# A conditioned mixture of experts on one core: seven pieces of work put in other places

## The chip, the core and the metric

The kernel runs on one core of a Trainium2 chip. The time is the device time of one execution in microseconds (us), and the aim is a smaller one. The core has five engines, each with its own queue that it works through in order: PE (TensorE, the matrix products), ACT (ScalarE), DVE (VectorE), POOL (GpSimd) and SP (SyncE, which here only issues transfers). They wait for one another through semaphores. A matrix product consists of a weight load (PEld) and the product itself (PE).

## What is computed

1024 tokens of 256 features are first conditioned: a dense 256x256 product, to which a low-rank product (rank 16, one of eight adapters per sequence of 32 tokens) is added. Behind it a mixture of eight experts works on the result, two experts for each token.

```python
def cond(x, W, A, Bm, scalings, adapter_idx):      # x: (32, 32, 256)
    H = jnp.einsum('btd,od->bto', x, W)
    xa = jnp.einsum('btd,brd->btr', x, A[adapter_idx])
    delta = jnp.einsum('btr,bor->bto', xa, Bm[adapter_idx])
    return H + delta * scalings[adapter_idx][:, None, None]

def ffn(x, w_gate, w1, w2, w3):                    # E = 8, H = 256, I = 704
    routing = softmax_integer(xf @ w_gate.T)       # fixed-point table of exp
    top_w, top_i = jax.lax.top_k(routing, 2)
    combine = zeros.at[arange(T)[:, None], top_i].add(top_w / top_w.sum(-1, keepdims=True))
    for e in range(E):
        h = jax.nn.silu(xf @ w1[e].T) * (xf @ w3[e].T)
        out = out + combine[:, e:e + 1] * (h @ w2[e].T)

out = x + ffn(cond(x, ...), ...)
```

## The kernel before

**Precision.** Products are made from a value split in two: a high part in a rounded 32-bit form and a low part, the rest. A product is hi·lo + hi·hi + lo·hi. ACT makes the high parts by copies (`copy`, L559, one line for all of them), DVE or POOL the low parts by a subtraction. So each operand passes ACT, then DVE (or POOL), then PE.

**First stage (to some 30 us).** PE makes the adapter products, the router's logits (two halves of 512 tokens) and turns them; DVE picks two experts for each token (a chain of small instructions, L767 to L782, whose ninth sets `picked_ready`). The conditioned rows are made in eight tiles of 128 tokens, `base(t)` (six matmuls: four at L1076, two at L1082) and `low_rank(t)` (three, L1093 to L1095); two tiles make a batch, which ACT copies out (`c_copy`) and stores (L574). Between the batches PE counts the picks ahead of each token, the ranks (one matmul at L1151, eight at L1155). From the ranks DVE makes the positions of the rows (L787 to L815), and PE the source of each row (L1179). Rows are grouped by expert into 23 slots of 128. Slot 0 is gathered by matmuls (`first_rows`, L1170); for slots 1 to 22 POOL issues indirect loads (`gather`, L460), the first when DVE has written `src_i` (L835).

**Second stage, the slots.** Each slot has three items i = 3s + j. PE's order for an item: `gate_up(i)` (L1210 four times, L1219 twice), then for one j the turn of the next slot's rows (`turn_slot(s + 1)`, L1188, two transposes that wait for that slot's gather), `turn_hidden(i - 1)` (L1226), `down(i - 2)` (L1247 to L1249; L1241 and L1242 in a slot's last). `turned_at(s)` gives j = 1 for all slots but slot 1, which `LATE_SLOTS` puts at j = 2. Behind a turn ACT makes `xs_hi` and DVE `xs_lo` (L876), and the first product of the next slot waits for both. From slot 1 on the expert's address is a register; ahead of each such product stand register instructions on PE's queue. For each item ACT makes silu (L613, or L617 and L618), DVE the product `hid` (L890, or L895 and L897), ACT `h_hi` and DVE `h_lo` (L905). A slot's result lies in one bank, `ya`; DVE copies it out (`slot_out`, L911, semaphore `y_out`), and the first `down` of the next slot waits for that.

**Weights.** SP loads an expert's weights in three pieces into `raw` (L390; experts 1 and 3 go to other places). For expert 0 the high parts are `expert_hi(0, k)` on ACT and the low parts `first_lo` (L726, piece 0 in halves) and `expert_lo` (L859) on DVE. The first halves of `raw` are free for expert 2 when these are done (`raw_free`).

**The tail.** Slots 0 to 20 are scattered by POOL to DRAM (`scatter`, L482, the s-th not before item s + 43 has its `hid`; `destinations()`, L842 to L852 on DVE, makes the targets) and come back token by token: SP waits for all scatters and issues four loads (L416). ACT scales the first choice (`scale_first`, L638), DVE adds the second (`mix`, L922), PE transposes the sum into the output banks (L1277). Slots 21 and 22 go another way: ACT and DVE split their scaled result (`direct_hi`, L644, and the same `slot_out`, L914), and PE multiplies it with a 0/1 matrix `hot_out`, which POOL makes (L550, two instructions, semaphore `places_ready`) (L1264). DVE adds x (L1010, four instructions) and SP stores (L420, four transfers).

The parts of this order that the change touches are all written out by hand: no scheduler moves them.

## Time and profile before

| | |
|---|---|
| time, median of 3 runs | 202.05 us (201.3 to 202.57) |
| the profiled execution | 201.05 us, of it span 199.3 us |
| PE busy | 192.5 us (97%) |
| PEld, POOL, DVE, ACT busy | 169.6, 130.3, 108.2, 82.5 us |
| chain that ended last | PE 86%, DMA 5%, DVE 4%, issue 1%, SPq 1%, ACT 1% |
| granted clock of PE | 0.997 |

The span runs from the first to the last instruction; 1.75 us of the profiled execution lie around it. A timeline row gives start, length (both us), engine, line, operation, tiles, count, and in brackets how long the engine had been idle and what ended that. Ends of matmuls are modelled and overlap the next one's start, so spacing is read from starts. "issue" is idle time in which nothing that the profile shows was waited for.

### The profile page before, as it was taken

Reading aid. Unit: us, or ns where it says so; the run is one execution under the profiler, and the core shown is the slowest. Engines: PE = TensorE matmul, PEld = TensorE weight load, DVE = VectorE, ACT = ScalarE, POOL = GpSimd, SP = SyncE. Lnnn points to the kernel's source line nnn. Section 1 sums busy time; section 2 is a strip of 40 time slices with the busy share of each in tenths; the row PEclk is TensorE's granted clock in tenths of the full one; section 3 lists DMA queues with packets and bytes.
Section 4 is the critical chain, followed back from the end, with each engine's and each line's share of the span. In section 5 each row is a group of like instructions: output and inputs, shape, how many; then the busy total and the mean of one; then the engine's idle time right before and its main releaser. Section 6 shows DMA issues by size and latency. Waiting matters only on the chain.

```text
span 199.3 us, 3883 instructions
## 1 busy us (share of the span) xinstructions
PE 192.5 (97%) x1209; PEld 169.6 (85%) x1209; DVE 108.2 (54%) x308; ACT 82.5 (41%) x225; POOL 130.3 (65%) x116
## 2 busy tenths in 40 slices
PE   7998999989999999999999999999999999999992
PEld 6677998778899888989988998899889889988861
DVE  0777898874545644435443553345675435543673
ACT  3756583587643323432333333234323333332740
POOL 8300008569898699999999999998544455418500
PEclk9999999999999999999999999999999999999998
DMA  4999522999993114183364356007312111101915
GB/s 130 348 378 386 189 105 68 333 356 361 359 361 117 58 53 132 48 277 99 109 201 169 109 192 189 13 3 250 120 54 54 54 61 60 67 30 53 358 41 212
DMA packets 14419, 32.67 MB, mean 164 GB/s; under 512 B 2400, under 2 KB 7648, under 8 KB 14272
## 3 DMA queue, kind: packets, MB, share of 16 engines
q1 hardware_dynamic: 11008, 25.70, 37.9%
q0 software_dynamic: 2128, 5.64, 8.8%
q10 hardware_dynamic: 1264, 1.07, 1.6%
q8 instruction: 12, 0.20, 0.4%
q14 instruction: 7, 0.06, 0.1%
HBM read 25.45 MB, written 6.96 MB: 163 GB/s over the span
## 4 chain that ended last, share of the span: by engine, by line
PE 86%; DMA 5%; DVE 4%; issue 1%; SPq 1%; ACT 1%; ACTq 0%; DVEq 0%; POOL 0%; POOLq 0%
PE gu L1210 27%; PE gu L1219 14%; PE ya L1247 7%; PE ht L1226 7%; PE ya L1248 6%; PE ya L1249 6%; DMA rows<-expert_rows 4%; PE ya L1018 3%; PE xt L1188 2%; PE gu L1076 2%; DMA expert_rows<-rows,dst_i 1%; PE ya L1242 1%; PE ya L1241 1%; PE gu L1264 1%; PE ya L1170 1%
## 5 line engine op out<-in xcount | busy, mean ns | idle before, releaser
L1210 PE MATMUL gu<-w_all,xs_hi 128*128 (+2 forms) x276 | 70.7, 377 | 0.3 <-issue 0.3
L890 DVE TENSOR_TENSOR hid<-gu,sg 128x256 f32<-128x256 f32 x46 | 19.5, 424 | 62.2 <-ACT sg L613 62.1
L1210 PEld LDWEIGHTS gu<-w_all,xs_hi 128*128 128x128 f32 x276 | 46.7, 188 | 4.8 <-issue 0.5
L613 ACT ACTIVATE sg<-gu 128x256 f32<-128x256 f32 x46 | 17.7, 385 | 73.2 <-PE gu L1219 73.2
L466 POOL TENSOR_TENSOR w_all<-raw,w_all 128x1024 fp32r<-128x1024 f32 (+2 forms) x14 | 43.9, 3147 | 3.8 <-DVE w_all L872 3.7
L460 POOL DMA_INDIRECT rows<-cond_rows,src_i x22 | 24.4, 1109 | 27.4 <-DVE src_i L835 22.9
L1219 PE MATMUL gu<-w_all,xs_lo 128*128 (+1 forms) x138 | 40.5, 375 | 0.0
L1247 PE MATMUL ya<-w_all,h_hi 128*128 (+1 forms) x115 | 38.4, 334 | 0.6 <-DVE rows L911 0.5
L482 POOL DMA_INDIRECT expert_rows<-rows,dst_i x21 | 20.3, 965 | 22.8 <-DVE hid L890 12.0
L1248 PE MATMUL ya<-w_all,h_hi 128*128 (+1 forms) x115 | 32.5, 283 | 0.0
L1249 PE MATMUL ya<-w_all,h_lo 128*128 (+1 forms) x115 | 32.3, 281 | 0.0
L1219 PEld LDWEIGHTS gu<-w_all,xs_lo 128*128 128x128 f32 x138 | 25.6, 188 | 3.9
L905 DVE TENSOR_TENSOR h_lo<-ht,h_hi 128x256 fp32r<-128x256 f32 x69 | 28.6, 414 | 0.0
L559 ACT ACTIVATE h_hi<-ht 128x256 fp32r<-128x256 f32 x69 | 26.7, 387 | 0.0
L1226 PE MATMUL ht<-ident,hid 128*128 128x128 f32 x138 | 26.3, 272 | 0.0
L1247 PEld LDWEIGHTS ya<-w_all,h_hi 128*128 128x128 f32 x115 | 21.7, 189 | 2.6 <-issue 1.5
L1226 PEld LDWEIGHTS ht<-ident,hid 128*128 128x128 f32 x138 | 18.6, 140 | 4.0
L1248 PEld LDWEIGHTS ya<-w_all,h_hi 128*128 128x128 f32 x115 | 21.9, 190 | 0.0
L1249 PEld LDWEIGHTS ya<-w_all,h_lo 128*128 128x128 f32 x115 | 21.7, 189 | 0.0
L515 POOL CAST w_all<-raw 128x1024 fp32r<-128x1024 f32 (+2 forms) x12 | 16.8, 1398 | 0.8 <-POOLq L510 0.8
L617 ACT ACTIVATE sg<-gu 128x128 f32<-128x128 f32 x23 | 6.4, 279 | 23.0 <-PE gu L1219 23.0
L895 DVE TENSOR_TENSOR hid<-gu,sg 128x128 f32<-128x128 f32 x23 | 6.7, 292 | 13.7 <-ACT sg L618 13.6
(192 smaller groups left out, 260.7 us busy)
## 6 DMA issues: line engine op xcount, KB each, us to landing
raw<-expert_weights SPq DMA_DIRECT2D x6, 896.0 KB, 4.8
raw<-expert_weights SPq DMA_DIRECT2D x6, 640.0 KB
raw<-expert_weights SPq DMA_DIRECT2D x6, 512.0 KB, 4.8
expert_rows<-zeros SPq DMA_DIRECT2D x1, 2048.0 KB, 14.4
rows<-expert_rows SPq DMA_DIRECT2D x4, 512.0 KB, 5.3
x<-x_t SPq DMA_DIRECT2D x4, 256.0 KB, 4.6
cond_rows<-c_rows ACTq DMA_DIRECT2D x4, 256.0 KB, 2.1
raw<-x_t SPq DMA_DIRECT2D x1, 1024.0 KB, 4.9
```

Source lines behind the costliest of these rows:

```text
L460: nc.gpsimd.indirect_dma_start(out=rows[:, s, :], out_offset=None, in_=c_dram[:, :], in_offset=bass.IndirectOffsetOnAxis(ap=src_i[:, s:s + ...
L466: return nc.gpsimd.tensor_tensor(lo_part(e, cols), from_raw(e)[:, cols], as_f32(hi_part(e, cols)), ALU.subtract)
L482: nc.gpsimd.indirect_dma_start(out=y_dram[:, :], out_offset=bass.IndirectOffsetOnAxis(ap=dst_i[:, s:s + 1], axis=0), in_=rows[:, s, :], in ...
L559: return nc.scalar.activation(out, in_, ACT.Copy)
L890: nc.vector.tensor_tensor(hid[i % HBUFS][:, :].rearrange("p (a b) -> p a b", b=P), bank[:, :].rearrange("p (a k b) -> p a k b", k=2, b=P)[ ...
L905: nc.vector.tensor_tensor(h_lo[i % HBUFS][:, :], ht[i % 2][:, 0:2 * P], as_f32(h_hi[i % HBUFS][:, :]), ALU.subtract).then_inc(h_lo_ready, 1)
L1210: nc.tensor.matmul(out, stay_hi[:, kc * P:(kc + 1) * P], moving(at, part + first + kc * P, n), start=kc == 0 and part == HI_COLS, stop=False)
L1219: last = nc.tensor.matmul(out, stay_lo[:, kc * P:(kc + 1) * P], moving(at, first + kc * P, n), start=False, stop=kc == KC - 1)
L1226: last = nc.tensor.transpose(ht[i % 2][:, q * P:(q + 1) * P], hid[i % HBUFS][:, q * P:(q + 1) * P], ident[:, :])
L1247: nc.tensor.matmul(out, stay_hi, w_l, start=j == q == 0, stop=False)
L1248: nc.tensor.matmul(out, stay_hi, w_h, start=False, stop=False)
L1249: last = nc.tensor.matmul(out, stay_lo, w_h, start=False, stop=False)
```

## The change

1. **Ranks.** `base(3)` is issued ahead of the rank matmuls on PE, not behind them.
2. **Expert 0.** On ACT the high part of piece 0 is made ahead of the router's weights; piece 1 is split in two (`SECOND_PARTS`, 1024 and 768 columns, with a semaphore of its own, `second_hi_ready`), the first ahead of the second half's `xa_hi`, the second where the whole piece stood. On DVE the first half of piece 0's low part goes ahead of `xa_lo(1)`, and the first part of piece 1's goes ahead of the routing chain; the 768 columns stay where the 1792 stood. `highs_of` counts the high parts, one fewer, for the other waits.
3. **Slot 1's turn.** `LATE_SLOTS` is empty: slot 1 is turned at j = 1 like the others, on PE, ACT and DVE.
4. **Destinations.** `destinations()` moves from item 3 to item 46 on DVE.
5. **`hot_out` of slot 21** is made ahead of the last scatter on POOL, that of slot 22 behind it as before.
6. **The eviction of slot 22.** On ACT `direct_hi(22)` goes ahead of `scale_first(2)`; on DVE `mix(2)` goes behind `slot_out(22)`.

```diff
@@ -34,6 +34,8 @@
+SECOND_PARTS = [slice(2 * ITEM_COLS, 4 * ITEM_COLS), slice(4 * ITEM_COLS, DOWN_AT)]
 HI_PIECES = [PIECES[0], PIECES[1], slice(DOWN_AT, HI_COLS)]
@@ -67,7 +69,7 @@
-LATE_SLOTS = (1,)
+LATE_SLOTS = ()
@@ -278,6 +280,7 @@
         raw_free = [sem(f"raw_free{k}") for k in range(len(PIECES) - 1)]
+        second_hi_ready = sem("second_hi_ready")
         second_ready = sem("second_ready")
@@ -344,6 +347,10 @@
             return 0 if e in (STAGED, STAGED_LOW) else e - (e > STAGED) - (e > STAGED_LOW)
+        def highs_of(e, k):
+            return len(PIECES) * e + k + 1 - (e > 0 or k > 0)
@@ -490,14 +497,14 @@
                 for k in range(len(PIECES) - 1):
-                    pool.wait_ge(whi_ready, len(PIECES) * e + k + 1)
+                    pool.wait_ge(whi_ready, highs_of(e, k))
                     ins = low(e, k)
...
                     fetch(e, n)
-                pool.wait_ge(whi_ready, len(PIECES) * (e + 1))
+                pool.wait_ge(whi_ready, highs_of(e, 2))
                 pool.wait_ge(third_ready, e - 1)
@@ -534,7 +541,16 @@
+            def make_places(l):
+                nc.gpsimd.tensor_scalar(hot_out[:, l, :], tokens, place[:, l:l + 1], None,
+                                        ALU.is_equal).then_inc(places_ready, 1)
             for s in range(SENT):
+                if s == SENT - 1:
+                    pool.wait_ge(pool_step, 4)
+                    for l in range(DIRECT - 1):
+                        make_places(l)
                 pool.wait_ge(hid_done, s + PACE)
@@ -545,10 +561,7 @@
-            pool.wait_ge(pool_step, 4)
-            for l in range(DIRECT):
-                nc.gpsimd.tensor_scalar(hot_out[:, l, :], tokens, place[:, l:l + 1], None,
-                                        ALU.is_equal).then_inc(places_ready, 1)
+            make_places(DIRECT - 1)
@@ -565,6 +578,10 @@
                     copy(hi_part(e, HI_PIECES[k]), from_raw(e)[:, HI_PIECES[k]]).then_inc(whi_ready, 1)
+            def first_hi_part(cols):
+                act.wait_ge(raw_in[1], RAW_LOADS[1])
+                copy(hi_part(0, cols), raw[:, cols]).then_inc(second_hi_ready, 1)
@@ -586,16 +603,17 @@
             copy(xa_hi[0][:, :], xa[0][:, :]).then_inc(xa_hi_ready, 1)
+            expert_hi(0, 0)
             act.wait_ge(g_done, 1)
...
             copy(g_both[:, :, 0:EXPERTS], g_at.rearrange("p (c e) -> p c e", e=EXPERTS)).then_inc(g_hi_ready, 1)
+            first_hi_part(SECOND_PARTS[0])
             act.wait_ge(xa_masked, 2)
             copy(xa_hi[1][:, :], xa[1][:, :]).then_inc(xa_hi_ready, 1)
-            expert_hi(0, 0)
             for h in range(HALVES):
...
                 copy(logits[:, tok_of(h)], logits_at[h]).then_inc(logits_out, 1)
-            expert_hi(0, 1)
+            first_hi_part(SECOND_PARTS[1])
             c_copy(0)
@@ -677,8 +695,8 @@
+            direct_hi(SLOTS - 1)
             scale_first(2)
-            direct_hi(SLOTS - 1)
             scale_first(3)
@@ -723,6 +741,11 @@
                 dve.wait_ge(whi_ready, 1)
+                return nc.vector.tensor_tensor(lo_part(0, cols), raw[:, cols], as_f32(hi_part(0, cols)), ALU.subtract)
+            def second_piece_lo(n):
+                cols = SECOND_PARTS[n]
+                dve.wait_ge(second_hi_ready, n + 1)
                 return nc.vector.tensor_tensor(lo_part(0, cols), raw[:, cols], as_f32(hi_part(0, cols)), ALU.subtract)
@@ -748,9 +771,10 @@
             mask_part(1)
+            first_lo(0)
             xa_lo_part(1)
-            first_lo(0)
             first_lo(1).then_inc(raw_free[0], 1)
+            second_piece_lo(0)
@@ -855,7 +879,7 @@
                 cols = PIECES[k]
-                dve.wait_ge(whi_ready, len(PIECES) * e + k + 1)
+                dve.wait_ge(whi_ready, highs_of(e, k))
                 return nc.vector.tensor_tensor(lo_part(e, cols), from_raw(e)[:, cols], as_f32(hi_part(e, cols)),
@@ -863,7 +887,7 @@
             def second_lo(n):
-                dve.wait_ge(whi_ready, len(PIECES) * STAGED + (1 if n < 2 else 2))
+                dve.wait_ge(whi_ready, highs_of(STAGED, 0 if n < 2 else 1))
                 return nc.vector.tensor_tensor(lo_part(STAGED, parts[n]), stage[:, parts[n]],
@@ -960,7 +984,7 @@
-            expert_lo(0, 1).then_inc(raw_free[1], 1)
+            second_piece_lo(1).then_inc(raw_free[1], 1)
             tokens_of_rows()
@@ -990,18 +1014,17 @@
                 if i == 3:
-                    destinations()
                     expert_lo(1, 2)
...
                     slot_out(s - 1)
+                if i == SHARES_AT - 1:
+                    destinations()
                 if SHARES_AT <= i < SHARES_AT + SHARE_PARTS:
                     weights_of_choices(i - SHARES_AT)
-                if i == ITEMS:
-                    mix(2)
+            mix(2)
             mix(3)
@@ -1144,6 +1167,7 @@
             base(2)
+            base(3)
@@ -1157,7 +1181,6 @@
-            base(3)
             low_rank(2)
```

PE's queue around the ranks, first before (from the end of `base(2)` to the start of `base(3)`), then now (from the end of `base(3)` to the start of `low_rank(2)`); `ht` holds the ranks, `gu` the conditioned rows:

```order
L1082 MATMUL gu<-pk_lo,x_hi 128x256 x2
L1151 MATMUL ht<-picked,before 128x64 [waits picked_ready,consts_ready]
L1155 MATMUL ht<-picked,ones 128x64
L1155 MATMUL ht<-picked,ones 128x56
L1155 MATMUL ht<-picked,ones 128x48
L1155 MATMUL ht<-picked,ones 128x40
L1155 MATMUL ht<-picked,ones 128x32
L1155 MATMUL ht<-picked,ones 128x24
L1155 MATMUL ht<-picked,ones 128x16
L1155 MATMUL ht<-picked,ones 128x8
L1076 MATMUL gu<-pk_hi,x_hi 128x256
```

```order
L1105 MATMUL gu<-pk_lo,x_hi 128x256 x2
L1175 MATMUL ht<-picked,before 128x64 [waits picked_ready,consts_ready]
L1179 MATMUL ht<-picked,ones 128x64
L1179 MATMUL ht<-picked,ones 128x56
L1179 MATMUL ht<-picked,ones 128x48
L1179 MATMUL ht<-picked,ones 128x40
L1179 MATMUL ht<-picked,ones 128x32
L1179 MATMUL ht<-picked,ones 128x24
L1179 MATMUL ht<-picked,ones 128x16
L1179 MATMUL ht<-picked,ones 128x8
L1116 MATMUL gu<-pk_hi,xa_hi 128x256
```

The six matmuls of `base(3)` now stand ahead of the wait for `picked_ready`, and nothing of the batch's base is left behind it.

PE's queue in slot 0 behind the products of item 1, before and now; `xt` is the turned slot, `ht` the turned hidden values:

```order
L1219 MATMUL gu<-w_all,xs_lo 128x512 x2
L1226 MATMUL ht<-ident,hid 128x128 [waits hid_done]
L1226 MATMUL ht<-ident,hid 128x128
L1210 MATMUL gu<-w_all,xs_hi 128x384 [waits c_out]
L1210 MATMUL gu<-w_all,xs_hi 128x384 x3
L1219 MATMUL gu<-w_all,xs_lo 128x384 x2
L1188 MATMUL xt<-ident,rows 128x128 [waits rows_in1]
L1188 MATMUL xt<-ident,rows 128x128
L1226 MATMUL ht<-ident,hid 128x128 [waits hid_done]
L1226 MATMUL ht<-ident,hid 128x128
```

```order
L1242 MATMUL gu<-w_all,xs_lo 128x512 x2
L1211 MATMUL xt<-ident,rows 128x128 [waits rows_in1]
L1211 MATMUL xt<-ident,rows 128x128
L1249 MATMUL ht<-ident,hid 128x128 [waits hid_done]
L1249 MATMUL ht<-ident,hid 128x128
L1233 MATMUL gu<-w_all,xs_hi 128x384 [waits c_out]
L1233 MATMUL gu<-w_all,xs_hi 128x384 x3
L1242 MATMUL gu<-w_all,xs_lo 128x384 x2
L1249 MATMUL ht<-ident,hid 128x128 [waits hid_done]
L1249 MATMUL ht<-ident,hid 128x128
```

The turn, which waits for the first gather (`rows_in1`), has moved ahead of item 0's `turn_hidden` and of item 2's products. On DVE, items 3 and 4, before (from item 2's `h_lo` to slot 0's copy out) and now:

```order
L905 TENSOR_TENSOR h_lo<-ht,h_hi 128x256 [waits h_hi_ready]
L842 TENSOR_SCALAR second<-code 128x24 [waits dve_step]
L844 SCALAR_TENSOR_TENSOR spare<-code,spare_row 128x24
L846 SCALAR_TENSOR_TENSOR dst_i<-code,spare 128x24 [waits dve_step]
L850 SCALAR_TENSOR_TENSOR place<-code,second 128x2
L852 TENSOR_SCALAR share_at<-code 128x2
L859 TENSOR_TENSOR w_all<-rows,w_all 128x1280 [waits whi_ready]
L872 TENSOR_TENSOR w_all<-rows,w_all 64x256
L890 TENSOR_TENSOR hid<-gu,sg 128x256 [waits silu_done]
L876 TENSOR_TENSOR xs_lo<-xt,xs_hi 128x256 [waits xs_hi_ready]
L905 TENSOR_TENSOR h_lo<-ht,h_hi 128x256 [waits h_hi_ready]
L911 COPY rows<-ya 128x256 [waits down_done]
```

```order
L929 TENSOR_TENSOR h_lo<-ht,h_hi 128x256 [waits h_hi_ready]
L883 TENSOR_TENSOR w_all<-rows,w_all 128x1280 [waits whi_ready]
L896 TENSOR_TENSOR w_all<-rows,w_all 64x256
L914 TENSOR_TENSOR hid<-gu,sg 128x256 [waits silu_done]
L900 TENSOR_TENSOR xs_lo<-xt,xs_hi 128x256 [waits xs_hi_ready]
L929 TENSOR_TENSOR h_lo<-ht,h_hi 128x256 [waits h_hi_ready]
L935 COPY rows<-ya 128x256 [waits down_done]
```

The five instructions of `destinations()` are gone from between item 3 and expert 1's last piece.

ACT's queue at the end, before (from the last `h_hi`) and now; L644, now L662, is the eviction of slot 22, L638, now L656, the scaling:

```order
L559 ACTIVATE h_hi<-ht 128x256 [waits ht_done]
L638 ACTIVATE rows<-rows,weight 128x256 [waits y_in1]
L638 ACTIVATE rows<-rows,weight 128x256
L644 ACTIVATE w_all<-ya,share 128x256 [waits share_in,down_done]
L638 ACTIVATE rows<-rows,weight 128x256 [waits y_in1]
L638 ACTIVATE rows<-rows,weight 128x256
```

```order
L572 ACTIVATE h_hi<-ht 128x256 [waits ht_done]
L662 ACTIVATE w_all<-ya,share 128x256 [waits share_in,down_done]
L656 ACTIVATE rows<-rows,weight 128x256 [waits y_in1]
L656 ACTIVATE rows<-rows,weight 128x256
L656 ACTIVATE rows<-rows,weight 128x256 [waits y_in1]
L656 ACTIVATE rows<-rows,weight 128x256
```

The eviction stands ahead of the two scalings that wait for the loads of `y_in1`.

## Rows read from the trace of the kernel before

**Rows 1.** Waits of PE, whole span: us in total, times, longest
```profile
PE ht L1151 <- DVE picked L779: 0.7, 1, 0.7
PE ya L1247 <- DVE rows L911: 0.5, 1, 0.5
```

**Rows 2.** Timeline, PE behind the ranks, 20 to 21 us
```profile
20.09 0.36 PE L1076 MATMUL gu<-pk_hi,x_hi 128*128 128x256 f32 x1
20.29 0.28 PE L1076 MATMUL gu<-pk_hi,x_lo 128*128 128x256 f32 x1
...
20.89 0.27 PE L1093 MATMUL gu<-pk_hi,xa_hi 128*128 128x256 f32 x1
```

**Rows 3.** Timeline, slot 0 into slot 1, 33 to 37 us, three engines
```profile
33.48 0.38 PE L1226 MATMUL ht<-ident,hid 128*128 128x128 f32 x2
...
33.70 0.81 SPq L390 DMA_DIRECT2D raw<-expert_weights  x2
...
35.23 0.39 ACT L559 ACTIVATE xs_hi<-xt 128x256 fp32r<-128x256 f32 x1
...
35.78 0.28 PE L1249 MATMUL ya<-w_all,h_lo 128*128 128x256 f32 x1
...
36.39 1.19 PE L1210 MATMUL gu<-w_all,xs_hi 128*128 x4 [0.33 <-issue]
```

**Rows 4.** Timeline, PE, slot 2 into slot 3, 49 to 52 us
```profile
50.69 0.28 PE L1249 MATMUL ya<-w_all,h_lo 128*128 x1
50.81 1.10 PE L1210 MATMUL gu<-w_all,xs_hi 128*128 x4
```

**Rows 5.** Timeline, DVE and PE, items 3 to 5, 39 to 44 us
```profile
39.16 0.17 DVE L842 TENSOR_SCALAR second<-code 128x24 f32<-128x24 f32 x1
...
39.70 1.48 DVE L859 TENSOR_TENSOR w_all<-rows,w_all 128x1280 fp32r<-128x1280 f32 x1
...
42.28 0.38 PE L1226 MATMUL ht<-ident,hid 128*128 128x128 f32 x2
...
42.43 0.40 DVE L911 COPY rows<-ya 128x256 f32<-128x256 f32 x1
...
43.18 0.38 PE L1247 MATMUL ya<-w_all,h_hi 128*128 x1 [0.52 <-DVE rows L911]
```

**Rows 6.** Timeline, the tail, 190 to 197 us, three engines
```profile
190.99 0.28 PE L1242 MATMUL ya<-w_all,h_lo 128*128 x1
...
191.18 0.91 ACT L638 ACTIVATE rows<-rows,weight 128x256 f32<-128x256 f32 x2 [1.57 <-DMA rows<-expert_rows]
...
191.99 0.46 ACT L644 ACTIVATE w_all<-ya,share 128x256 fp32r<-128x256 f32 x1
...
192.50 2.20 PE L1264 MATMUL gu<-w_all 128*128 128x512 f32 x8 [0.35 <-ACT w_all L644]
...
193.71 1.28 DVE L1010 TENSOR_TENSOR raw<-gu,raw 128x512 f32<-128x512 f32 x2
...
195.50 1.29 DVE L1010 TENSOR_TENSOR raw<-gu,raw 128x512 f32<-128x512 f32 x2 [0.52 <-PE gu L1277]
```

**Rows 7.** Line L420, the first two output transfers, issued 0.6 us apart
```profile
DMA to landing us min/median/max: 2.1/2.1/2.1
```

**Rows 8.** Timeline, DVE and POOL around slot 20's end, 180 us
```profile
180.21 0.29 DVE L895 TENSOR_TENSOR hid<-gu,sg 128x128 f32<-128x128 f32 x1 [0.67 <-ACT sg L618]
...
180.32 0.96 POOL L482 DMA_INDIRECT expert_rows<-rows,dst_i  x1 [5.19 <-DVE rows L911]
```

**Rows 9.** Timeline, ACT, around the second half's xa_hi, 12 to 15 us
```profile
12.18 0.19 ACT L559 ACTIVATE g_both<-ya 128x24 fp32r<-128x24 f32 x1 [1.30 <-PE ya L1066]
13.48 0.63 ACT L559 ACTIVATE xa_hi<-xa 128x512 fp32r<-128x512 f32 x1 [1.10 <-DVE xa L711]
14.02 1.05 ACT L559 ACTIVATE w_all<-raw 128x1024 fp32r<-128x1024 f32 x1
```

**Rows 10.** Line L390, expert 0's second piece, issued at 4.1 us
```profile
DMA to landing us min/median/max: 8.3/8.3/8.3
```

## The prediction

> **What bounds the kernel.** I read the share of busy time first: PE is busy for 192.5 of the 199.3 us span, at a granted clock of 0.997, so there is nothing to win in the clock, and little except where PE stands idle, before its first and after its last product, or in work that is not done at all. No part of the change removes work from PE. The list of PE's waits comes second. Two of its entries stand beside lines of the diff [rows 1]: 0.7 us, once, in front of the ranks (L1151), and 0.5 us, once, in front of the first `down` of slot 1 (L1247). The timelines around the edited lines come third. They show two more losses: a slot's first product that starts late with "issue" ahead of it [rows 3], and the tail, where PE stands 0.35 us in front of the last direct product and DVE 0.52 us between two pairs of additions [rows 6]. Between the start of slot 1 and the tail the slots run at PE's pace, so time won before them shifts all of them, and the tail's end with them.
>
> The sum is made against the profiled execution (201.05 us: 199.3 of span and 1.75 around it). The median of the runs is 1.00 above that; I carry the differences over to the median.
>
> **1. The ranks.** Before, PE waits 0.7 us for `picked_ready` [rows 1], makes the ranks and then the six matmuls of `base(3)`. These start at 20.09, the next piece of work (`low_rank(2)`) at 20.89: 0.80 us [rows 2]. Five of the six spacings, from 20.29 to 20.89, are 0.12 each. The first is 0.20, and I take its 0.08 over 0.12 for the restart behind the small rank matmuls, which `low_rank(2)` will now pay. So 6 x 0.12 = **0.72** moves ahead of the wait, and the idle stretch of 0.7 takes it up: the ranks start when `picked` is there, as before, and all behind them is 0.72 earlier. Bounds: 0.80 if no restart is paid, 0.6 if the six run 0.1 beyond the moment of `picked`. What follows on the way to slot 0 starts from the ranks and from PE: the positions on DVE follow the ranks, the copies of the conditioned rows follow PE's third and fourth tiles. DVE has less to do there than before, since 768 columns of expert 0's low part stand where 1792 stood. By 1.48 us for 1280 columns [rows 5] that is 0.9 against 2.1 us.
>
> **2. Expert 0's pieces.** Nothing waits for expert 0's weights before, so these edits gain nothing by themselves; the question is whether they are covered. Piece 0's high part (1024 columns) takes 1.05 us [rows 9] and goes into ACT's idle stretch of 1.30 us ahead of the router's weights at 12.18 [rows 9]. The second piece was asked for at 4.1 us and lands 8.3 later [rows 10], at 12.4. Its 1024 columns are then copied from 12.4 to some 13.4, in the idle 1.10 ahead of `xa_hi` at 13.48 [rows 9]. That leaves 0.1 us. On DVE, by the rate of step 1, the first half of piece 0's low part (512 columns, 0.6 us) goes into the idle stretch in which it waited for that same `xa_hi`, and the 1024 columns (1.2 us) into the time that PE takes over the logits. One more instruction on either engine, 0.1 to 0.2 us, lies beside PE's work. I cost it all at 0. If the cover is missing, `xa_hi`, the logits, `picked` and everything else are late by what is missing: 0 to 0.2 at the row's landing time.
>
> **3. Slot 1's turn.** Before, the first product of slot 1 starts at 36.39 and ends its four at 37.58; the product ahead of it starts at 35.78, 1.80 earlier [rows 3]. In an undisturbed slot the same stretch, from 50.69 to 51.91, is 1.22 [rows 4]. So 1.80 - 1.22 = 0.58 is lost there. `xs_hi` of slot 1 was ready at 35.23 + 0.39 = 35.62 [rows 3], before PE wanted it. What ate the time is "issue": the register instructions that pick the expert stand behind the wait for `xs_hi`, so they can't be run ahead. With the turn one item earlier they can, as in slot 2. That gives back 0.58. The price: the turn now stands where `turn_hidden(0)` stood, at 33.48, and its gather has landed by 33.70, when SP, which waits for that gather too, issues its next load [rows 3]. That is a wait of 0.22, and with a refill of 0.08 (as in step 1) 0.30. Queued behind it on PE are `turn_hidden(0)` and item 2's products, and nobody else is called on by then. Net 0.58 - 0.30 = **0.28**. The gather starts from `src_i`, which follows the ranks, so I take it to move with step 1. If it did not move at all, the wait would be 0.22 + 0.72 and the net -0.44; if it were there at PE's call, +0.58.
>
> **4. Destinations.** The five instructions stand from 39.16 to 39.70 on DVE [rows 5], 0.54 us, ahead of expert 1's last piece and so of slot 0's copy out at 42.43, for which PE waited 0.52 at 43.18 [rows 5]. PE also lost a refill of 0.10 there (0.38 for a first matmul against 0.28 in rows 3). DVE is not idle from 39.16 to that copy, so the copy comes 0.54 earlier, which removes the wait: **0.62** with the refill. PE calls for the copy 0.28 earlier than DVE's chain otherwise moves, but part of that chain is started by PE and moves as well, so the fit is close. Bounds: 0.45 (0.2 of a wait is left) to 0.70. At item 46 the 0.54 lie in an idle stretch of 0.67 such as DVE has in every slot's third item [rows 8], at no cost to PE. The scatters then begin some 3 us later than now, with POOL's instruction at 0.96 [rows 8] against more than 2 us for an item, so they catch up within eight.
>
> **5. Places.** `hot_out` of slot 21, half of POOL's pair of instructions at the end and about 2.9 us long, goes into the 5.19 us in which POOL waits ahead of its last scatter [rows 8]. PE does not wait on these places in the list of its waits. Worth 0, with more room than before.
>
> **6. The eviction of slot 22.** Before, ACT scales two tiles from 191.18 and makes `direct_hi(22)` only at 191.99, though its `down` ended at 190.99 + 0.28 = 191.27. PE's last direct product waits for it and starts at 192.50 [rows 6]. Now the eviction starts at about 191.3, 0.7 earlier. PE's idle 0.35 goes, and so does some 0.16 by which the modelled end of the matmul ahead of it overstates (0.28 long where the next starts after 0.12 [rows 2]), and a refill of 0.1: PE is 0.6 earlier. That is more than the 0.52 for which the third addition waited, so DVE becomes the engine that ends last: `y_lo`, four sums, then four additions of 0.6 each (1.28 for two with a modelled end) [rows 6] without the gap. ACT's last two scalings end as before, since its three pieces of work are only put in another order; the sums, of which two now stand behind `y_lo`, I let end 0.04 later. So **0.48**. Bounds: 0.1 if the sums come 0.4 late, 0.7 if the whole of ACT's gain arrives.
>
> **Sum.** 0.72 + 0 + 0.28 + 0.62 + 0 + 0.48 = 2.10. The span becomes 197.2, the profiled execution 198.95, and the median 202.05 - 2.10 = **199.95 us**, 1.04% less. About 1% (2.0 us) is what a measurement of this kernel can tell from no change, so the forecast lies on that border.
>
> **Rivals.**
>
> *Output transfers back up* (against step 6). Four transfers of 262,144 bytes would now leave 0.6 apart. The first two did so before, and each landed 2.1 us after its issue [rows 7], the second no later than the first, which speaks against a queue. If the later two were slowed by 0.13 each time, the last would be 0.39 late and step 6 worth 0.09: 202.05 - 1.71 = 200.35. The Trainium skill, "Perfetto Trace Analysis", section "Engine Utilization", gives 358 GB/s of memory bandwidth as a core's share, an estimated 0.73 us for such a transfer, which would give this rival; the same section lets a core that runs alone reach some 120% of it, an estimated 0.61. The trace agrees with the latter as far as two transfers show.
>
> *The gather does not follow the ranks* (against step 3). Its issue runs through DVE and POOL; were DVE's chain held by the weights' low parts, the wait at the turn would grow by the 0.72, and step 3 be -0.44: a gain of 1.38, 200.65. For it: the landing is only 0.22 behind the call. Against it: DVE has less ahead of the positions than before.
>
> *DVE is late with slot 0's copy all the same* (against step 4): the wait on `y_out` is PE's calling earlier, and 0.6 of the 0.62 comes back as a wait. Gain 1.5, 200.55.
>
> *The ranks do not come earlier* (against step 1): the copies behind PE, or `base(3)` overrunning `picked`, keep 0.7 of it. Gain 1.4, 200.65.
>
> *Slower:* the second piece lands late. ACT's queue holds `xa_hi` of the second half behind a wait for that load, and its landing is known from one execution [rows 10]. Every microsecond beyond 12.5 delays the logits, `picked` and the rest by as much; beyond 14.6 it eats the 2.10, and 4.2 beyond that slack the kernel is at 204.15. Against it: other transfers of that time are issued unchanged.
>
> **How the numbers follow.** Forecast 0.64 (its own range 199.3 to 200.6, from the bounds of steps 1 to 6 taken not all at once, and the scatter of the runs); gather 0.10; copy out 0.08; output queue 0.08; ranks 0.06; slower 0.04. The partial cases end at 200.35 to 200.65. The range 198.9 to 201.3 takes them in with the runs' own scatter above (0.5 to 0.75 by their highest and lowest); below, it takes in the case in which steps 1, 3, 4 and 6 reach their upper bounds (0.08 + 0.30 + 0.08 + 0.22 = 0.68 more, 199.27) with some of that scatter. The border of 1%, 200.03, cuts the forecast's own range from 199.3 to 200.6 almost in the middle; steps that reach more than I take weigh as much as those that reach less, so I give 0.40 of its 0.64 to the side below. Of the four partial cases (0.32) 0.07 fall below the border by scatter, 0.25 above. So faster by over 1% 0.47, within 1% 0.24 + 0.25 = 0.49, slower 0.04.
>
> **What would show it.** Step 1: no wait of PE on `picked`, or less than 0.1, and ranks that start as before while `low_rank(2)` comes 0.7 earlier. Step 2: `xa_hi` of the second half no later than 13.5. Step 3: no "issue" ahead of item 3's first product, and a wait of 0.2 to 0.3 at the turn. Step 4: no wait on slot 0's copy out. Step 6: the eviction of slot 22 directly behind the last `down`, and four additions without a gap. The prediction falls if a wait that is not in the list today appears between 12 and 45 us, or if the additions keep their gap.

## The result: 1% slower, with a new wait at 143 us

The changed kernel takes 203.51 us (median of 4 runs, 203.03 to 205.35) where the kernel before takes 202.03: a ratio of 1.0101, 95% interval 1.0059 to 1.0144. I had forecast 199.95, with a range up to 201.3.

| | before | after |
|---|---|---|
| the profiled execution | 201.05 us, span 199.3 | 203.03 us, span 201.3 |
| PE busy | 192.5 us | 193.0 us |
| slots 16 and 17 together (start to start) | 13.85 us | 16.94 us |
| slot 0, slot 1 | 5.76, 7.51 us | 5.62, 6.95 us |
| end of the last `down` to the end of the last addition | 5.52 us | 5.02 us |

Slot times are distances between the starts of the first low products (L1219, now L1242) of one slot and the next.

The waits of PE, whole span (us in total, times, longest), are other ones than in [rows 1]:

```profile
PE ya L1270 <- issue: 1.7, 1, 1.7
PE ya L1041 <- POOL zeros L432: 1.0, 1, 1.0
PE ht L1249 <- DVE hid L921: 0.9, 1, 0.9
```

The waits on the picks and on slot 0's copy out are gone. The first and third of these rows are new, and they stand next to each other, in slots 16 and 17. The starts of slots 16, 17 and 18, from PE's timeline:

```profile
139.43 0.62 PE L1242 MATMUL gu<-w_all,xs_lo 128*128 x2
...
148.13 0.62 PE L1242 MATMUL gu<-w_all,xs_lo 128*128 x2
...
156.37 0.62 PE L1242 MATMUL gu<-w_all,xs_lo 128*128 x2
```

These slots take 8.70 and 8.24 us, where before they took 6.94 and 6.91: 3.09 us lost. At 139.43 the changed kernel is still 1.00 us ahead of the kernel before (140.43). What happens there, from the timelines of PE, DVE, ACT and POOL:

```profile
143.13 0.28 PE L1265 MATMUL ya<-w_all,h_lo 128*128 x1
...
143.76 0.96 POOL L489 DMA_INDIRECT expert_rows<-rows,dst_i  x1 [0.30 <-issue]
143.96 0.52 PE L1242 MATMUL gu<-w_all,xs_lo 128*128 x2
...
145.71 0.42 DVE L935 COPY rows<-ya 128x256 f32<-128x256 f32 x1 [1.70 <-remote]
...
146.38 0.38 PE L1270 MATMUL ya<-w_all,h_hi 128*128 x1 [1.68 <-issue]
...
148.61 0.28 ACT L635 ACTIVATE sg<-gu 128x128 f32<-128x128 f32 x1 [5.11 <-remote]
```

DVE's copy of the slot's result needs PE's last `down`, which ended at 143.13 + 0.28 = 143.41. It starts at 145.71. ACT's silu needs the low products that ended at 143.96 + 0.52 = 144.48. It starts at 148.61, 4.1 us later. Both engines were idle and had nothing else to wait for. So PE's work is done, and the word of it comes late; the waits list calls such a releaser "remote". Ends of matmuls are modelled, but PE works in order, and at 148.13 it had started the low products of the next item, while ACT still waited for those before them. PE then waits for DVE and ACT in its turn. The Trainium skill, "Perfetto Trace Analysis", section "Per-engine timelines", says that the profile shows an instruction's execution and not the way of its semaphore update to the others. The trace agrees: PE's rows show nothing, and the 4.1 us appear only in the idle time of the receivers.

At the same time POOL issues scatters without a pause, seven of them with starts from 138.62 to 146.28 and some 1.26 us apart. In the kernel before the scatters began at 135.86. Moving the destinations to item 46 made them begin 2.8 us later, and the owed ones follow in a row. This is the theory that the experiments test: **scatters that follow one another without a pause make PE's signals late (A)**. Its rival: the gap belongs to that moment of the program, whatever the scatters do (B).

### The profile page after: what moved, and what is told of

It reads as the page before. It is cut to its first block, busy times and chain, and to the rows that moved or that the text cites. A ratio compares the mean times of both kernels' runs of the same rounds, so it can differ in the third digit from the quotient of the medians.

```text
span 201.3 us, 3885 instructions
## 1 busy us (share of the span) xinstructions
PE 193.0 (96%) x1209; PEld 169.2 (84%) x1209; DVE 108.6 (54%) x309; ACT 83.3 (41%) x226; POOL 129.5 (64%) x116
## 3 DMA queue, kind: packets, MB, share of 16 engines
HBM read 25.45 MB, written 6.96 MB: 161 GB/s over the span
## 4 chain that ended last, share of the span: by engine, by line
PE 82%; DMA 6%; DVE 4%; another core or an unknown queue 3%; ACT 2%; issue 1%; SPq 1%; DVEq 0%; POOLq 0%
PE gu L1233 27%; PE gu L1242 13%; PE ya L1270 7%; PE ht L1249 7%; PE ya L1271 6%; PE ya L1272 6%; DMA x<-x_t 3%; PE xt L1211 2%; DMA rows<-expert_rows 2%; PE gu L1099 2%; DVE rows L946 1%; DMA expert_rows<-rows,dst_i 1%; PE ya L1265 1%; PE ya L1264 1%; PE gu L1105 1%
## 5 line engine op out<-in xcount | busy, mean ns | idle before, releaser
L467 POOL DMA_INDIRECT rows<-cond_rows,src_i x22 | 23.5, 1069 | 27.0 <-DVE src_i L859 22.4
L1242 PE MATMUL gu<-w_all,xs_lo 128*128 (+1 forms) x138 | 40.6, 375 | 0.0
L1242 PEld LDWEIGHTS gu<-w_all,xs_lo 128*128 128x128 f32 x138 | 25.6, 188 | 3.9
L1249 PE MATMUL ht<-ident,hid 128*128 128x128 f32 x138 | 26.3, 272 | 0.9 <-DVE hid L921 0.9
L1249 PEld LDWEIGHTS ht<-ident,hid 128*128 128x128 f32 x138 | 18.5, 140 | 5.1 <-DVE hid L921 1.3
```

What stands on the lines that cost most here:

```text
L467: nc.gpsimd.indirect_dma_start(out=rows[:, s, :], out_offset=None, in_=c_dram[:, :], in_offset=bass.IndirectOffsetOnAxis(ap=src_i[:, s:s + ...
L1242: last = nc.tensor.matmul(out, stay_lo[:, kc * P:(kc + 1) * P], moving(at, first + kc * P, n), start=False, stop=kc == KC - 1)
L1249: last = nc.tensor.transpose(ht[i % 2][:, q * P:(q + 1) * P], hid[i % HBUFS][:, q * P:(q + 1) * P], ident[:, :])
```

## Experiments

### Undoing or moving the destinations

Changed kernel, destinations back at item 3 (e1), or at item 44 (e2); kernel before with destinations at item 46 and nothing else (e3).

```diff
# e1
                 if i == 3:
+                    destinations()
                     expert_lo(1, 2)
-                if i == SHARES_AT - 1:
-                    destinations()
# e2
-                if i == SHARES_AT - 1:
+                if i == SHARES_AT - 3:
                     destinations()
# e3, the kernel before
                 if i == 3:
-                    destinations()
                     expert_lo(1, 2)
+                if i == SHARES_AT - 1:
+                    destinations()
```

> The changed kernel with the destinations back at item 3 on DVE. Its trace shows two gaps in which PE's slots 16 and 17 take 8.70 and 8.24 us where the others take 6.8, 3.3 us together; there seven scatters follow one another 1.26 us apart. Theory A (the late destinations press the scatters together, and the burst delays what PE's neighbours wait for): no such gap, slots 16 and 17 at 6.8 to 6.95, and back comes the wait of 0.5 us on slot 0's copy out. Time 203.5 - 3.3 + 0.6 = 200.8. Theory B (the gap belongs to that moment of the program and would be there whatever the destinations do, for instance with PE's instruction load): the gap stays, 204.1.

> The changed kernel with the destinations at item 44, two items earlier, so that POOL finds them when it has finished the weights, as before the change. Theory A: the first scatters start some 136 us into the span and no longer follow one another at 1.26 us more than three times; no gap in slots 16 and 17, no wait on slot 0's copy out, 200.2 us. Theory B: the gap stays, 203.5.

> The kernel before with one edit: the destinations at item 46. Theory A: the wait on slot 0's copy out goes (0.6), the gap of some 3.3 us comes: 202.0 - 0.6 + 3.3 = 204.7. Theory B (the gap comes from the phase of the other edits): 201.4, no gap.

Measured: e1 201.54 us (ratio 0.9985, 0.9952 to 1.0017), e2 201.72 (0.9975, 0.9948 to 1.0003), e3 204.81 (1.0137, 1.0068 to 1.0206). e3 came out as theory A had it: one edit, slot 1 at 6.96 instead of 7.51 (0.55 won), and slot 16 at 10.83. Its "remote" waits:

```profile
ACT sg L617 <- remote: 3.9, 1, 3.9
...
DVE rows L911 <- remote: 1.3, 1, 1.3
```

So the gap needs none of the other six edits. Not all of e3's 4.0 us is the wait: PE stood idle for 2.44 us up to 148.09, and behind that its granted clock is 0.50 from 148 to 151 us, the lower of its two levels (1.2 GHz). The products from there to slot 17's first low product take 3.15 us, where the same ones take 1.75 in the changed kernel (146.38 to 148.13, clock 1.00, behind an idle time of 1.68). So some 1.4 us are the clock. But e1 and e2 missed: both still have a gap, slot 16 at 7.98 and 8.81. In both, five scatters stand in a row (135.26 to 140.40, and 135.66 to 140.85). As I had put it, that was harmless, since the kernel before does nearly the same.

e2 has a second defect. Its destinations, on DVE, against what POOL does then:

```profile
131.94 2.69 DVE L866 TENSOR_SCALAR second<-code 128x24 f32<-128x24 f32 x1
132.85 1.77 DVE L868 SCALAR_TENSOR_TENSOR spare<-code,spare_row 128x24 f32<-128x24 f32 x1
```

```profile
125.92 6.98 POOL L473 TENSOR_TENSOR w_all<-raw,w_all 128x1792 fp32r<-128x1792 f32 x2
132.84 0.77 POOL L478 TENSOR_TENSOR w_all<-raw,w_all 64x256 fp32r<-64x256 f32 x1
133.57 1.01 POOL L541 IOTA iota_r<- 128x1024 uint16 x1
```

The first, 0.17 us long in [rows 5], takes 2.69 here, the second 1.77, until POOL's last one ends at 134.58.

### The kernel before, traced again

> The kernel before, unchanged, for a second trace of it. The first profiled execution (201.05 us) lies 1 us under the median of its runs, and the runs scatter by 1% and more. If PE's signals are sometimes late in the kernel before too, while POOL issues scatters without a pause, one of the slots 15 to 17 takes some 1 us longer than 6.8 here; if the kernel before is free of it, all slots take 6.8 to 6.95 as in the first trace.

Measured: 201.53 us, slot 16 at 7.78, and a "remote" wait that the first trace does not have:

```profile
ACT sg L613 <- remote: 3.4, 1, 3.4
```

Five scatters in a row stand there (135.83 to 140.99). The first trace, on which I had built the sum, had six (135.86 to 142.27) and lost at most 0.12 (slot 16 takes as long, 6.94 and 6.98, in the two kernels g2 and g1 below, which have no such row). So the loss is no fixed price of the row of scatters: it may fall out small. The kernel before pays it in some of its executions, and the profiled one was among the lucky ones.

### Fewer scatters in a row, or a row elsewhere

The first six scatters between POOL's weight pieces of experts 6 and 7: in the changed kernel with destinations at item 20 (f3), and in the kernel before (f4). f5 is f3 with scatters 6 to 9 held until item 53.

```diff
# f3, f4
                         fetch(e, 2 + 2 * k)
+                    if e >= EXPERTS - 2:
+                        scatter(3 * (e - EXPERTS + 2) + k)
...
-            for s in range(SENT):
+            for s in range(6, SENT):
# f3 also
-                if i == SHARES_AT - 1:
+                if i == 20:
                     destinations()
# f5, against f3
-                pool.wait_ge(hid_done, s + PACE)
+                pool.wait_ge(hid_done, max(s + PACE, 54) if s < 10 else s + PACE)
```

> The changed kernel with the destinations at item 20, and the first six scatters put between POOL's weight pieces of experts 6 and 7 (some 105 to 131 us), so that the other fifteen go at most one for each item. Theory A (scatters that follow one another without a pause make PE's signals late): no slot from 15 to 21 over 6.95 us, and all the steps of the prediction are left: span about 197.5, time 199.5 to 200. If the late signals have another cause, one of the slots 15 to 21 is still 1 to 2 us long: 201.5.

> The kernel before with the same six scatters between POOL's weight pieces and nothing else (destinations at item 3 as they were). If some runs of the kernel before lose time to late signals, this takes it away: 201.1 and a narrower scatter. If the kernel before is free of it, 202.0.

> f3_early with one edit: the scatters 6 to 9 are held until item 53, so that scatters 6 to 10 and those behind them follow one another without a pause at some 153 to 165 us, at another place of PE's program than before. Theory A: the gap moves with the burst, 1 to 4 us are lost in the slots 17 to 20, time 201 to 204. If the gap belongs to slot 16 of the program, nothing is lost here: as f3_early.

Measured: f3 208.05 us (1.0316, 1.0290 to 1.0342), f4 206.87 (1.0232, 1.0186 to 1.0279), f5 214.07 (1.0575, 1.0518 to 1.0632). All times missed, f3 (with f5, which contains it) and f4 by mechanisms of their own. In f3 slot 7 takes 14.69 us, since DVE's destinations stand still behind POOL:

```profile
77.44 9.18 DVE L870 SCALAR_TENSOR_TENSOR spare<-code,spare_row 128x24 f32<-128x24 f32 x1
```

```profile
78.05 6.87 POOL L473 TENSOR_TENSOR w_all<-raw,w_all 128x1792 fp32r<-128x1792 f32 x2
84.88 0.72 POOL L478 TENSOR_TENSOR w_all<-raw,w_all 64x256 fp32r<-64x256 f32 x1
85.54 1.03 POOL L522 CAST w_all<-raw 128x1024 fp32r<-128x1024 f32 x1
```

In f4 the six scatters make the last expert's weights late (`PE ya L1249 <- POOL w_all L471: 3.6`), and slot 15 takes 11.73. In both of these long slots the granted clock fell as well (means of 0.77 and 0.89).

Slots 15 to 22 still answer the question. In f3, with the later scatters about 2.3 us apart and no more than three indirect transfers in a row (a load of shares among them), every slot from 15 to 21 takes 6.81 to 6.93, and 208.05 less the 7.88 of slot 7 is 200.2. In f5 seven scatters stand in a row (162.18 to 169.87), a load of shares behind them, and slots 18 and 19 take 9.79 and 8.21 while slot 16 takes 7.01. (f5's span is 6.0 longer than f3's: 4.4 in these two slots, at mean clocks of 0.90 and 0.91, and 1.6 ahead of slot 0, where its clock fell as it does in g4 below.) The gap went where the row of scatters went. Theory B falls: f5's waits,

```profile
ACT sg L637 <- remote: 5.3, 1, 5.3
...
DVE rows L937 <- remote: 2.0, 1, 2.0
```

The instruction load, which e1's expectation names under B, is answered by the kinds of the transfers: in the gaps of e1 (138 to 142.5 us), e2, h2 and f1 (138 to 143) and e3 (142 to 149.4) no instructions are loaded. One load of 16 KB falls into the gap of the change, and one runs in g1 between 140 and 150 us without a loss.

### Pace against place

Two edits of the changed kernel, both together (g1) and each alone (h1 with its own even rule, h2), the rule alone in the kernel before (g2), and a first try at spreading (e4).

```diff
# g1, g2
-                pool.wait_ge(hid_done, s + PACE)
+                pool.wait_ge(hid_done, PACE + 2 + (18 * s + 16) // 20)
# g1, h2
-                if i == SHARES_AT - 1:
+                if i == SHARES_AT - 2:
                     destinations()
# h1
-                pool.wait_ge(hid_done, s + PACE)
+                pool.wait_ge(hid_done, PACE + 3 + (17 * s + 10) // 20)
# e4
-                pool.wait_ge(hid_done, s + PACE)
+                pool.wait_ge(hid_done, s + PACE + max(0, 4 - s // 4))
```

> The changed kernel with two edits: the destinations at item 45, when POOL reads no weights any more, and a rule by which scatter s waits for the hid of item 45 + (18 s + 16) // 20, so that the scatters go evenly at not more than one for each item but for two pairs. Theory A (scatters that follow one another without a pause make PE's signals late, and nothing else is wrong with the change): no slot from 15 to 21 over 6.95 us, the scatters' end as before, span 197.5 to 198, time 199.5 to 200. If one of these slots is still long: 201 to 202.

> The changed kernel with one edit: scatter s waits for the hid of item 46 + (17 s + 10) // 20, so that the scatters start as late as in the change but go evenly, with pairs only. The destinations stay at item 46. Theory A (the back-to-back scatters, not the late start): no slot from 15 to 21 over 6.95 us, time 199.8 to 200.2. If the late start is what costs: 201 or more.

> The changed kernel with the other edit alone: the destinations at item 45, the scatters as in the change. About five or six scatters follow one another without a pause, some 136 to 142 us. Theory A: a loss of 0.1 to 2 us in slot 16, as in the kernels that start their scatters at that time, 200.5 to 202. If the place of the destinations alone is what counts, none: 199.9.

> The kernel before with the same rule for the scatters and nothing else. The second trace of the kernel before had its slot 16 at 7.78 us, behind five scatters in a row; the first had 6.94. Theory A: the even scatters take such losses away, 201.1 to 201.5 and less scatter between the runs. If they cost the kernel before nothing on the whole: 202.0.

> The changed kernel with the destinations at item 46 as in the change, but the scatters spread: the s-th waits for the hid of item s + 43 plus 4 for the first four, plus 3 for the next four, and so on down to nothing from the 17th, so five go in four items and not seven in a row. Theory A (the burst, not the lateness): no gap, 200.2. If the lateness itself or the moment makes the gap, it stays: 203.5.

| kernel | longest row of indirect transfers without a pause | us lost in slots 15 to 21 | time, ratio (95%) |
|---|---|---|---|
| g1 | 3 | none (6.80 to 6.98) | 199.88, 0.9898 (0.9862 to 0.9934) |
| g2 | 3 | none (6.78 to 6.94) | 201.01, 0.9962 (0.9940 to 0.9985) |
| h1 | 5, a load of shares among them, 157.16 to 162.24 | 1.5 in slot 19 | 201.23, 0.9969 (0.9952 to 0.9986) |
| h2 | 5, 135.72 to 140.92 | 2.0 in slot 16 | 201.72, 0.9988 (0.9967 to 1.0009) |
| e4 | 5, twice, a load of shares in each, 159.68 to 164.79 and 168.01 to 173.10 | 0.2, 0.3 in slots 16, 17; 0.5, 1.2 in slots 20, 21 | 202.01, 0.9987 (0.9959 to 1.0014) |

g1 came out as theory A had it (slot 16, at 6.98, 0.03 over the limit that I had set), and is faster than both kernels. All that PE waited for in the whole span is in its first stage:

```profile
PE ya L1041 <- POOL zeros L432: 1.0, 1, 1.0
PE ht L1054 <- ACT x_hi L572: 0.8, 1, 0.8
```

Its scatters around the longest row:

```profile
152.90 0.96 POOL L489 DMA_INDIRECT expert_rows<-rows,dst_i  x1 [1.13 <-DVE hid L921]
154.16 0.96 POOL L489 DMA_INDIRECT expert_rows<-rows,dst_i  x1 [0.30 <-issue]
155.42 0.96 POOL L489 DMA_INDIRECT expert_rows<-rows,dst_i  x1 [0.30 <-issue]
157.62 0.96 POOL L489 DMA_INDIRECT expert_rows<-rows,dst_i  x1 [1.24 <-DVE hid L914]
```

Three in a row cost nothing here (e4 has a row of three from 145.65 to 148.18 and 0.3 in slot 17). A row of five cost 0.5 to 2.0 us, seven times in six traces (e1, e2, f1, h1, h2, and e4 twice); seven in a row cost 3.1 to 4.4 in three (the change, e3, f5), of which the lower clock has a part in e3 and f5. The six of the first trace, at 0.12 or less, are the exception. The place of the destinations alone (h2) does not help, and the pace alone (h1, e4) helps only as far as it keeps its rows short: both of my first rules bunched the scatters up again around the loads of the shares, and lost there. So h1 missed its 199.8 to 200.2 by 1.0, and e4 its 200.2 by 1.8. By its expectation h1's 201.23 would speak for the rival that the late start is what costs. Its trace speaks against that: the scatters start at 138.41 there, as late as in the change, slots 15 to 18 take 6.81 to 6.93, and the loss stands in slot 19, behind the row of five. g2, 0.7 us faster than the kernel before, shows the price in that kernel's runs.

### The other steps

g1 with slot 1's turn in its old place (g3), and with `base(3)` behind the ranks (g4), one trace each.

```diff
# g3
-LATE_SLOTS = ()
+LATE_SLOTS = (1,)
# g4
             base(2)
-            base(3)
...
+            base(3)
             low_rank(2)
```

> g1_even with slot 1's turn back at the later place. The prediction's step 3 gives 0.28 for the earlier turn; the traces with it show slot 0 some 0.1 to 0.25 shorter. So slots 0 and 1 together should take 0.1 to 0.28 us more here than in g1_even (12.55 to 12.6 there).

> g1_even with base(3) behind the ranks again. Step 1 gives 0.72: the start of slot 0's first low product comes 0.7 us later against the start of the ranks' inputs on PE (the small products of the router) than in g1_even, and PE waits some 0.7 in front of the ranks.

Measured: in g3 slots 0 and 1 take 5.61 + 6.95 = 12.56 us, in g1 5.54 + 6.96 = 12.50. The earlier turn is worth 0.06 there, below what I expected. In g4 PE waits 0.7 in front of the ranks, and `low_rank(2)` starts 1.03 behind them where it is 0.23 in g1. That is 0.80 by the start of `low_rank(2)`. The whole time of g4 (202.14) says nothing on step 1: PE's granted clock was 0.51 for 3.4 us of its first stage, as its windows show (PE busy, ..., PEclk, DMA share, GB/s),

```profile
11.00:13.40 2.40, 2.40 (x16) 1.95 (x17) 1.82 (x4) 1.91 (x4) 0.00 (x0) 1.00 1.02 406
13.40:16.80 3.40, 3.40 (x10) 2.63 (x9) 3.27 (x5) 1.50 (x3) 0.00 (x0) 0.51 1.04 359
```

which cost some 1.5 us (10.71 us from the router's first small product to the ranks, 9.18 in g1). That is the lower of the clock's two levels, 1.2 GHz; PE had been busy throughout the 2.40 us ahead of it. f5's trace has the same fall (0.54 from 13.40 to 16.80), the other fourteen have none there. Why it fell stays open.

## Why the prediction was wrong

**Step 1, the ranks: right.** The ranks follow `base(3)` without a wait, and `low_rank(2)` follows the ranks:

```profile
20.15 0.19 PE L1175 MATMUL ht<-picked,before 128*128 128x64 f16 x1
20.18 0.35 PE L1179 MATMUL ht<-picked,ones 128*128 128x64 f16 x8
20.38 0.36 PE L1116 MATMUL gu<-pk_hi,xa_hi 128*128 128x256 f32 x1
```

From the router's first small product to slot 0's first low product the traces of the kernel before have 20.98 and 20.96, those of the change and of g1 20.26: 0.72, the number of the sum. It does not show in clock time, since the changed kernel's profiled execution was 0.30 late from its first loads on (10.97 against 10.67).

**Step 2, expert 0: right, with the margin as thin as said.** The wait for the second piece is a 0.19 us idle stretch of ACT, and `xa_hi` stands 0.36 later in the span than in [rows 9], of which 0.30 is the late start (so at 13.84 it missed the sign "no later than 13.5", by 0.06 of its own). The ranks lie 9.18 behind the router in both.

**Step 3, the turn: direction right, size wrong.** I took the 0.58 of [rows 3] for what the old place costs. The same stretch in g3 takes 0.45 from the last product to the next slot's first, with an idle time of 0.17 where [rows 3] have 0.61 and 0.33. Slot 0 takes 5.61 to 5.78 us in the six traces with the old place (mean 5.69) and 5.50 to 5.70 in the ten with the new one (mean 5.60). The step is worth about 0.1: [rows 3] were at the upper end of their scatter, as three of the six are (5.76 to 5.78; the others 5.61 and 5.62). The price of the new place, 0.30 in the sum, is about that: in the trace of the change the turn starts 0.17 us later behind the low products than `turn_hidden` did before (0.63 against 0.46) and takes 0.05 longer, and the first `down`, which the sum did not have, starts 0.25 behind the transposes ahead of it where it was 0.13. It is the gain of 0.58 that was too large: 0.48 against [rows 3] (0.61 less 0.13), 0.3 against g3.

**Step 4, the destinations: the part on the path right, the part called free wrong.** Slot 1 went from 7.51 to 6.95, 0.56 for the 0.62 of the sum (some 0.16 of the wait is left: the first `down` starts 0.29 behind the transposes, 0.13 in the next slot; and the refill of 0.10 was not to be won, since the first `down` takes 0.21 before and 0.22 now to the next). The step that failed is the sentence that the scatters "begin some 3 us later than now ... so they catch up within eight", which stands in the sum at no cost to PE. They did just that (2.8 us later, seven in a row), and the catching up is what cost 3.09. I had counted POOL's instructions and asked whether they were in time; I had not asked what several scatters in a row do to the others. The first trace gave no hint: it holds six in a row that cost 0.12 at most. A second trace of the same kernel would have shown 0.97. Nor did my signs of being wrong look there: they watch for new waits from 12 to 45 us and at the additions, and this one stands at 143.

**Step 5, the places: right.** No wait of PE names them.

**Step 6, the tail: right against its own trace, wrong as a gain.** 5.02 against 5.52 is the 0.48 of the sum, and the eviction stands where it was forecast:

```profile
193.61 0.47 ACT L662 ACTIVATE w_all<-ya,share 128x256 fp32r<-128x256 f32 x1 [1.69 <-PE ya L1265]
...
194.52 1.68 DVE L946 SCALAR_TENSOR_TENSOR rows<-rows,weight 128x256 f32<-128x256 f32 x4
196.12 2.47 DVE L1033 TENSOR_TENSOR raw<-gu,raw 128x512 f32<-128x512 f32 x4
```

The additions have no gap, and the output transfers did not back up (2.0 to 2.3 us to landing). But the old order takes 4.83 (f1), 4.84 (e3), 5.03 (f4), 5.36 (g2) and 5.52 in its five traces, the new one 5.01 to 5.03 in all of its traces. In the first trace the last loads of the scattered rows landed late, ACT's scalings with them ([rows 6], idle 1.57 on a DMA; 0.83 in f1). The new order takes the scatter away, and its mean gain is some 0.1.

**The sum.** 0.72 + 0.1 + 0.56 + 0.1 is about 1.5, some 0.6 less than the 2.10 of the forecast (steps 3 and 6 above all); the rest of the miss, and what turned the gain into a loss, is the 3.09 that belongs to no term. None of my rivals was it either; the slower one that I named (the second piece landing late) did not happen. That g1 takes the forecast time is partly luck: about 1.1 of its 1.85 us are the change's steps (g1 against g2, where the terms above add up to 1.5), and 0.7 is the loss that the kernel before had in its own runs (g2). The changed kernel's longest runs, 203.91 and 205.35, have a lower mean clock (0.992 and 0.983; 0.998 in the profiled one). In e3 a mean of 0.992 was one stretch at the lower level, worth 1.4 us, so the clock behind a longer gap can be the difference; they have no trace that would show it.

**What stays open.** Why PE's signals come late. The rows show when: for signals that PE gives from about the fourth transfer of a row on, by 1 to 5.5 us; ACT and DVE wait for PE's signals then, and for none of each other's. In seven traces the last of them arrives 1.0 to 1.4 us after the end of the row; in e4 and f5 one more, behind the row, is 1.5 to 1.6 late. The DMA engines are no bound then (slot 16's window has a DMA share of 0.30). The gathers are issued by the same kind of instruction: in the trace of the change five of them follow one another from 29.23 to 35.71, with 0.30 of idle time between them, and no wait on a "remote" signal stands there; this is one row of that length. Whether the writes to DRAM, the pace, or something that the recording adds makes the difference was not tried. The runs without a trace lose as much as the profiled ones, but each of them has a span and a clock on record too, so they do not rule the recording out.

## To carry to other kernels

Work that is moved off the critical path takes its followers along: ask not only whether they are still in time, but in what formation they arrive. A queue that is behind works off what it owes without a pause, and here that alone cost more than all the moved work had won. Pacing it evenly over the time that it has took 0.4% off the kernel before (g2), and with the destinations one item earlier brought the changed one from 1.0101 to 0.9898 of it (g1). And a loss read in one execution is a sample: two terms of this sum (slot 1's turn, the tail) were larger in the trace that they were read from than in others, and the price of the scatters was smaller.

## What the hardware showed beyond that

A tiny DVE instruction can wait for a whole chain of POOL's. `spare<-code,spare_row`, 0.18 us elsewhere, took 9.18 us behind four instructions of POOL's that read SBUF (f3), and in e2 two instructions of that size were held to 134.6, when POOL's chain ended. The Trainium skill, "SBUF — State Buffer", section "Who interferes with whom", has the rule: a DVE instruction with two SBUF inputs and a GpSimd instruction that reads SBUF exclude each other, and the later one blocks until the first is finished. f3 agrees that the two exclude each other, but not on the order: DVE's instruction started at 77.44, 0.61 ahead of the first of the four (78.05), and yet ended at 86.62, only when the last had (86.57); it did not get in between them. e2 goes beyond the rule as told here: `second<-code` has one input, and POOL's last instruction, the iota, only writes. What held the two there was not tried. At item 45 (h2) the same two take 0.26 and 0.18, when POOL's reading instructions are over.
